# Gate and up products as three one-pass terms of split weights and input

## What is computed

```python
w = lut[idx]                                   # lut: 16 values; idx: gate, up 1376x512, down 512x1376
h = silu(x_norm @ gate.T) * (x_norm @ up.T)    # 512 positions x 1376
x = x + h @ down.T
# scan, 512 channels, 16 states, 512 steps:
state = state * exp(delta_t * A) + (delta_t * u_t) * B_t
y_t   = sum_n state[n] * C_t[n]
```

## Time and profile before

| | |
|---|---|
| median of the runs | 2582.32 us |
| the profiled execution, its own time | 2584.38 us |
| its span, first to last instruction | 2582.6 us |
| mean granted TensorE clock | 0.937 |
| busy: TensorE, VectorE, GpSimd, ScalarE | 2262.6, 1771.1, 1052.6, 920.4 us |
| window attention, about | 59 to 930 us |
| feed-forward with the scan, about | 1198 to 1865 us |

### The profile page before, as it was taken

The page is one execution under the profiler, slowest core; times in us unless marked ns, Lnnn a source line. Parts: engine busy times, 40 slices in busy tenths (PEclk is TensorE's granted clock), DMA queues, the critical chain, the costliest instruction groups (busy, mean ns, idle before and its releaser), DMA issues. The chain is left out here.

```text
span 2582.6 us, 24445 instructions
## 1 busy us (share of the span) xinstructions
PE 2262.6 (88%) x6992; PEld 1049.2 (41%) x6992; DVE 1771.1 (69%) x2979; ACT 920.4 (36%) x1759; POOL 1052.6 (41%) x789
## 2 busy tenths in 40 slices
PE   6998998999899777774798989989869999999858
PEld 3554444455455443332243434334333333434224
DVE  1887687688768877773688897987745455554454
ACT  1443323334333323331554636446203323232311
POOL 2453333355333424443598888988700000000033
PEclk9999999999999988886899999999979999999878
DMA  6000000000000022225321222221142222121021
GB/s 245 18 21 17 17 25 21 17 17 21 21 17 25 22 88 82 82 82 198 116 91 53 86 83 82 91 77 62 49 131 50 50 49 49 40 58 34 16 98 53
DMA packets 88746, 158.34 MB, mean 61 GB/s; under 512 B 14912, under 2 KB 42432, under 8 KB 86352
## 3 DMA queue, kind: packets, MB, share of 16 engines
q1 hardware_dynamic: 72256, 139.76, 17.1%
q10 hardware_dynamic: 15888, 17.43, 2.1%
q0 software_dynamic: 512, 0.13, 0.0%
HBM read 101.18 MB, written 30.80 MB: 51 GB/s over the span
## 5 line engine op out<-in xcount | busy, mean ns | idle before, releaser
L1389 PE MATMUL c_bank<-c_xn_t,c_weights 128*128 128x512 f32 (+1 forms) x704 | 326.4, 609 | 21.1 <-ACT c_h_t L1429 19.5
L706 POOL TENSOR_SCALAR a_prob<-a_prob,a_rsum 128x256 f32<-128x256 f32 x256 | 147.1, 594 | 466.8 <-DVE a_rsum L634 466.6
L1287 DVE TENSOR_TENSOR_SCAN s_state<-s_decay,s_state 128x512 f32<-128x512 f32 x256 | 305.0, 1210 | 36.1 <-ACT s_decay L1221 36.1
L1237 POOL TENSOR_TENSOR s_state<-s_b_rows,s_delta_u 128x1024 f32<-128x1024 f32 x128 | 301.2, 2363 | 11.2 <-DMA s_b_rows<-scan_bc 8.8
L1221 ACT ACTIVATE s_decay<-s_delta,s_a 128x512 f32<-128x512 f32 x256 | 173.2, 688 | 296.5 <-DVE s_state L1287 269.4
L438 PE MATMUL a_bank<-a_xn_t,a_wq 128*128 128x512 f32 x512 | 227.2, 592 | 0.0
L521 PE MATMUL a_bank<-a_wo,a_out_t 128*128 128x512 f32 x512 | 222.3, 592 | 0.0
L1910 POOL DMA_DIRECT2D d_qs<-d_neg_t x16 | 8.2, 514 | 515.3 <-DVE d_neg_t L1841 515.3
L549 ACT ACTIVATE a_prob<-a_score,a_neg_m 128x256 f32<-128x256 f32 x256 | 117.8, 476 | 278.8 <-DVE a_neg_m L629 278.6
L320 DVE TENSOR_SCALAR f_picks<-f_mask,f_lut_xor,f_lut 128x260 int32<-128x260 int32 x512 | 202.5, 468 | 9.6 <-DVE f_mask L314 1.1
L1762 ACT ACTIVATE d_prob_t<-d_score 128x512 f32<-128x512 f32 x256 | 139.0, 595 | 194.5 <-PE d_score L1645 193.2
(11 more groups left out here) (194 smaller groups left out, 3726.6 us busy)
## 6 DMA issues: line engine op xcount, KB each, us to landing
s_b_rows<-scan_bc SPq DMA_DIRECT2D x64, 512.0 KB, 3.6
f_idx<-in_idx SPq DMA_DIRECT2D x64, 130.0 KB, 2.1
ffn_weights<-f_picks SPq DMA_DIRECT2D x64, 130.0 KB, 1.8
r_factor<-in_factors SPq DMA_DIRECT2D x8, 1024.0 KB, 9.0
d_qs<-d_hi SPq DMA_DIRECT2D x128, 64.0 KB, 2.0
d_ks<-d_hi SPq DMA_DIRECT2D x128, 64.0 KB, 2.0
a_wo<-in_wo_t ACTq DMA_DIRECT2D x1, 4096.0 KB, 15.7
scan_y<-m_d_u SPq DMA_DIRECT2D x4, 1024.0 KB, 3.9
```

The lines of the kernel that those rows point to most:

```text
L1237: pool.tensor_tensor(self.state[:, s], row.broadcast_to([P, 2, T]), self.delta_u[:, h % 2], ALU.mult) \
L1287: dve.tensor_tensor_scan(self.state[:, s, e, :], self.decay[u % 2][:], self.state[:, s, e, :], 0.0, ALU.mult, ALU.add).then_inc(self.scann ...
L1389: mm = nc.tensor.matmul(banks[b][0:width[o], :], weights[:, lo:lo + width[o]], xn_t[:, k, :], start=(k == 0), stop=(k == KD - 1))
```

## The change

The lookup now stores every chunk three times: the weights, their part rounded to float32r (`f_hi`, a cast on ScalarE) and the remainder (`f_lo`, a subtraction on GpSimd). Chunks go alternately to two places; SyncE loads the indices of chunk n+1 behind the stores of chunk n-1. Gate and up indices are laid out tile by tile. In the feed-forward stage four slots hold the two parts of one gate and up tile; ScalarE issues the two loads of a tile three tiles ahead, behind silu, in every pass. Only the down weights stay in SBUF. The normalized input is split as well, a cast on ScalarE and a subtraction on VectorE per tile, and a fill is twelve one-pass products: high by high, high by low, low by high for each of four k. The next pass's normalization stands in pieces 8 and 12, among the fills, and its turning in the middle of the downs (piece 28). C of all passes is loaded and split once, into one 128-row tile.

```diff
-W_UP, W_DOWN = KD * INTER, 2 * KD * INTER
+W_DOWN = 2 * KD * INTER
...
+    STORES = 3 * 16
...
-        self.mask = sb("f_mask", [P, 4, CH], I32)
-        self.picks = sb("f_picks", [P, LUT // 2, CH], I32)
+        self.mask = sb("f_mask", [P, 3, CH], I32)
+        self.picks = sb("f_picks", [P, LUT // 2 + 1, CH], I32)
+        self.hi = sb("f_hi", [P, CH], F32R)
+        self.lo = sb("f_lo", [P, CH], F32R)
...
+    def turn(self, i, n):
+        return i * (self.PER_PASS // 2) + n // 2
+    def place(self, n):
+        return 0 if n % 2 == 0 else LUT // 2
+    def chosen(self, n):
+        return self.picks[:, self.place(n), :]
+    def scalar(self, act, i, n):
+        act.wait_ge(self.step_done, self.step_value(i, n, self.STEPS))
+        act.wait_ge(self.stored[1 - n % 2], self.turn(i, n + 1) * self.STORES + 1)
+        self.nc.scalar.copy(self.hi[:], self.chosen(n).bitcast(F32)).then_inc(self.rounded[n % 2], 1)
+    def gpsimd(self, pool, i, n):
+        pool.wait_ge(self.rounded[n % 2], self.turn(i, n) + 1)
+        self.nc.gpsimd.tensor_tensor(self.lo[:], self.chosen(n).bitcast(F32),
+                                     self.hi[:].bitcast(F32), ALU.subtract).then_inc(self.split[n % 2], 1)
...
     def sync(self, sp, i):
         def store(n):
-            sp.wait_ge(self.step_done, self.step_value(i, n, self.STEPS))
-            sp.dma_start(self.scratch["weights"][:, bass.ds(i * (self.PER_PASS * CH) + n * CH, CH)],
-                         self.picks[:, 0, :]).then_inc(self.stored, 16)
+            columns = bass.ds(i * (self.PER_PASS * CH) + n * CH, CH)
+            done = self.stored[n % 2]
+            sp.wait_ge(self.split[n % 2], self.turn(i, n) + 2)
+            sp.dma_start(self.scratch["weights"][:, columns], self.chosen(n)).then_inc(done, 16)
+            sp.dma_start(self.scratch["weights_hi"][:, columns], self.hi[:].bitcast(F32)).then_inc(done, 16)
+            sp.dma_start(self.scratch["weights_lo"][:, columns], self.lo[:].bitcast(F32)).then_inc(done, 16)
         for n in range(self.PER_PASS):
-            if n == 1:
-                sp.wait_ge(self.step_done, self.step_value(i, 0, 0))
-            elif n > 1:
-                sp.wait_ge(self.step_done, self.step_value(i, n - 2, 1))
+            if n:
+                sp.wait_ge(self.step_done, self.step_value(i, n - 1, 0))
...
+    def mask_of(self, n, bit):
+        return self.mask[:, bit, :] if bit < 3 else self.idx[:, n % 2, :]
...
             if j == 0:
-                dve.wait_ge(self.stored, (i * self.PER_PASS + n) * 16 + 1)
-            last = dve.tensor_scalar(picks[:, j, :], mask[:, 0, :], self.lut_xor[:, j:j + 1],
+                dve.wait_ge(self.stored[s], self.turn(i, n) * self.STORES + 1)
+            last = dve.tensor_scalar(picks[:, j or self.place(n), :], mask[:, 0, :], self.lut_xor[:, j:j + 1],
...
                     swap(*at, nxt[3:])
+                    lookup.scalar(act, i, g * TT)
                     take(("turn", g, 0, 0), i, prob_t[:, 0, 0, :])
                     take(("turn", g, 1, 0), i, prob_t[:, 1, 0, :])
                     take(("turn", g, 1, 1), i, prob_t[:, 1, 1, :])
@@ -591,6 +624,9 @@
                         if tt + 2 < TT:
                             for prev in range(2):
                                 take(("turn", g, tt + 2, prev), i, prob_t[:, tt % 2, prev, :])
+                        if tt % 2 == 0:
+                            lookup.scalar(act, i, g * TT + 1 + tt // 2)
+                    lookup.scalar(act, i, g * TT + 3)
...
+                    for n in range(TT):
+                        lookup.gpsimd(pool, i, g * TT + n)
...
+        for row in range(0, P, DS):
+            sp.dma_start(self.c_raw[row:row + DS, :], self.scratch["bc"][row // DS % B, DS:2 * DS, :]) \
+                .then_inc(self.c_in, 16)
...
+        n = c // 32 * DS + c % 16
+        self.nc.tensor.matmul(self.c_bank[c % 2][:], self.c_pick[:, n:n + 1].broadcast_to([P, P]),
+                              self.c_parts[:], start=True, stop=True).then_inc(self.c_spread, 1)
...
+    SLOTS = 4
+    w_parts = sb("c_w_parts", [P, SLOTS, 2, 2 * KD * P], F32R)
+    w_down = sb("c_w_down", [P, OT, D], F32)
...
-    xn_t = sb("c_xn_t", [P, KD, T], F32)
+    xn_parts = sb("c_xn_parts", [P, 2, KD, T], F32R)
...
+    PARTS = len(SPLIT)
+    XN_AT = FILLS + 2 * PARTS
+    PIECES = FILLS + TT * PARTS + 1
+    USES = OT + TT // 2 + KD // 2
+    STATS_AT, NORM_AT = 8, 12
...
+    def load_weights(eng, i, o):
+        n = i * OT + o
+        s, columns = n % SLOTS, slice(o * 2 * KD * P, o * 2 * KD * P + 2 * KD * width[o])
+        for part, name in enumerate(("weights_hi", "weights_lo")):
+            eng.dma_start(w_parts[:, s, part, 0:2 * KD * width[o]].bitcast(F32), scratch[name][:, columns]) \
+                .then_inc(w_in[s], 16)
...
-                for k in range(KD):
-                    lo = b * W_UP + k * INTER + o * P
-                    mm = nc.tensor.matmul(banks[b][0:width[o], :], weights[:, lo:lo + width[o]], xn_t[:, k, :],
-                                          start=(k == 0), stop=(k == KD - 1))
+                terms = [(k, w, x_) for k in range(KD) for w, x_ in ((0, 0), (0, 1), (1, 0))]
+                for k, w, x_ in terms:
+                    at = (b * KD + k) * width[o]
+                    mm = nc.tensor.matmul(banks[b][0:width[o], :], w_parts[:, n % SLOTS, w, at:at + width[o]],
+                                          xn_parts[:, x_, k, :],
+                                          start=((k, w, x_) == terms[0]), stop=((k, w, x_) == terms[-1]))
...
+                    elif j == XN_AT:
+                        if i + 1 < B:
+                            features(i + 1)
+                    else:
+                        down(i, *down_piece(j))
...
+            def load_ahead(n):
+                if n < B * OT:
+                    if n >= SLOTS:
+                        i, o = divmod(n - SLOTS, OT)
+                        act.wait_ge(full[1], fill_turn(i, o) + 1)
+                    load_weights(act, *divmod(n, OT))
+            for n in range(1, SLOTS):
+                load_ahead(n)
...
+                        if i * OT + j // 2 >= 1:
+                            load_ahead(i * OT + j // 2 + SLOTS - 1)
+                    if j == XN_AT and i + 1 < B:
...
+            def features(i):
+                for k in range(KD):
+                    dve.wait_ge(xn_rounded, i * KD + k + 1)
+                    nc.vector.tensor_tensor(xn_parts[:, 1, k, :], banks[k % 2][:], xn_parts[:, 0, k, :].bitcast(F32),
+                                            ALU.subtract).then_inc(free[k % 2], 1)
```

More of the change, by code:

```diff
@@ L262, in __init__ @@
         self.step_done = core.sem("f_step")
-        self.stored = core.sem("f_stored")
+        self.rounded = core.sems("f_rounded", 2)
+        self.split = core.sems("f_split", 2)
+        self.stored = core.sems("f_stored", 2)
     def load_table(self, sp):
@@ L291, in sync_end @@
     def sync_end(self, sp):
-        sp.wait_ge(self.stored, 16 * CHUNKS + 1)
+        for done in self.stored:
+            sp.wait_ge(done, self.STORES * (CHUNKS // 2) + 1)
     def vector_setup(self, dve):
-        start_at_one(dve, self.step_done, self.stored)
+        start_at_one(dve, self.step_done, *self.stored, *self.split)
         dve.wait_ge(self.lut_in, 16)
@@ L313, in pick @@
         for bit in range(1, 4):
-            last = dve.tensor_scalar(mask[:, bit, :], self.idx[:, s, :], 1 << bit, None, ALU.bitwise_and)
+            last = dve.tensor_scalar(self.mask_of(n, bit), self.idx[:, s, :], 1 << bit, None, ALU.bitwise_and)
         last.then_inc(self.step_done, 1)
@@ L329, in choose @@
             for j in range(0, LUT // 2, 2 * half):
-                last = self.nc.vector.copy_predicated(self.picks[:, j, :], self.mask[:, level + 1, :],
+                last = self.nc.vector.copy_predicated(self.picks[:, j or self.place(n), :], self.mask_of(n, level + 1),
                                                       self.picks[:, j + half, :])
@@ L1124, in load_half @@
         sp.dma_start(self.delta_u[:, s], self.scratch["delta_u"][i, :, own, :]).then_inc(self.delta_u_in[s], 16)
-        if h % 2 == 0:
-            if i:
-                sp.wait_ge(self.c_split, i)
-            for part in range(2):
-                sp.dma_start(self.c_raw[part * DS:(part + 1) * DS, :], self.scratch["bc"][i, DS:2 * DS, :]) \
-                    .then_inc(self.c_in, 16)
     def load_rows(self, sp, r):
@@ L1202, in scalar_setup @@
         act.wait_ge(self.pick_in, 16)
-        self.nc.scalar.copy(self.c_pick[:], self.pick_raw[:, 0:DS]).then_inc(self.picked, 1)
-        self.round_c(act, 0)
+        self.nc.scalar.copy(self.c_pick[:], self.pick_raw[:, 0:B * DS]).then_inc(self.picked, 1)
+        act.wait_ge(self.c_in, P // DS * 16)
+        self.nc.scalar.copy(self.c_hi[:], self.c_raw[:]).then_inc(self.c_rounded, 1)
         act.wait_ge(self.a_step, 2)
-    def round_c(self, act, i):
```

(33 more changed lines are left out.)

81 lines of the change are left out of this document (32 added, 49 removed).

## The result

| | |
|---|---|
| median of the runs after | 2609.72 us, four runs (2608.64 to 2611.96) |
| before, beside them | 2582.06 us (2578.64 to 2584.28) |
| ratio | 1.0109, 95% interval 1.0092 to 1.0127 |
| span of the profiled execution | 2606.9 us (before 2582.6) |
| mean granted TensorE clock | 0.927 (before 0.937) |

The changed kernel is slower by some 27 us. Two large amounts of opposite sign make that up. I read them from the first instruction of each stage: the context stage begins at 1028.0 in place of 930.6 us, so window attention takes **97.4 us more**. From the first statistics of the feed-forward stage to the first of the stage behind it are 615.3 us in place of 684.1, so that stage takes **68.8 us less**. The remaining stages together take 4.3 us less. Nothing was done to find out why.

A forecast was written before the change was run, and what follows sets the result against it. TensorE was taken as the bound, alternating with ScalarE in attention and matched by an equal scalar chain in feed-forward fills. 58 + 8 + 28 - 8 - 24 - 19 = +43 gave 2625 us for the median, range 2570 to 2670.

The forecast's parts named there:

- The new wait of ScalarE: Attention: ScalarE's cast of chunk 1 waits for VectorE and delays TensorE; +58 us in twelve groups, +8 in three normalizing ones.
- Clock: Attention: twelve new TensorE stalls are each followed by a lower granted clock, 2.3 us lost each, +28 us.
- The rest of the lookup: Attention: GpSimd's 64 subtractions and 128 more stores hide behind other work, costing nothing.
- One-pass fills: Feed-forward gate and up: TensorE saves 0.64 us per fill, but the scalar chain stays; -8 us, last pass only.
- one chain: Feed-forward fills: ScalarE's exp, table loads and silu, then the scans, hold a pair with two chunks at 8.1 us.
- Downs: Feed-forward downs of three passes: normalization leaves, 11 us less each, transposes cost 3 more; -24 us.
- start: Feed-forward start: fewer loads on ScalarE's queue ahead of the first decay, first fill some 4 us later; -19 us.
- C spread: Feed-forward: 128 rows in place of 32 stream the same 512 columns, one split replaces four; costed at nothing.
- A: Rival, attention: cast, subtraction, stores and index load close too late, so VectorE waits as well; 2670 us, chance 0.14.
- B: Rival, feed-forward fills: TensorE is the bound, so its saving is paid in full; 2562 us, faster, chance 0.09.
- C: Rival, attention: ScalarE's holds do not reach TensorE, only 64 casts cost time; 2556 us, faster, chance 0.08.
- D: Rival, fills: a one-pass product costs 0.43 us, weight loads not hidden; 2625 + 100 us, chance 0.05.

The follow-up runs named there:

- experiments 1 and 3: experiment 1, and as third the kernel before with ScalarE only waiting for chunks 1 and 2, no cast, subtraction or store added: 2664.36 us, ratio 1.0309.
- experiment 1: The changed kernel with the casts of chunks 1 to 3 of each group moved behind the group's last copy on ScalarE: 2535.89 us, ratio 0.9829.

## Why the prediction came out as it did

2625 us was forecast and 2609.7 measured: slower, as forecast, and inside the range. 43 us more was forecast, 27.7 measured. By its steps:

- **The new wait of ScalarE** (58 + 8). Right in place and kind, as experiments 1 and 3 show. TensorE's idle time grew by 68.2 us, against 66. The parts are less good than the sum. The hold, its cast included, was taken as 7.7 and 5.6 us by turns, and is about 7.6 in every plain group (645.74 to 653.32 in the one shown), of which TensorE feels 5.6 to 5.8; so the plain groups cost 68.5 us in place of 58. The three others cost 28.7, less the 19.6 of late adds: 9, against 8. Against that stand 11.8 us less of waits for GpSimd's probabilities, which the prediction did not have. So the close sum is in part luck.
- **Clock** (+28). 27.9 us more of busy TensorE for the same work. The mechanism is in the rows behind the hold; the size per hold was 2.7 us in the one shown, against 2.3, and there were fifteen holds and not twelve, while stalls of before went. That the total agrees is luck too. Idle time and clock together, 68.2 + 27.9 = 96.1, are the 96 us by which the window of the stage grew.
- **The rest of the lookup** (nothing). Wrong: the step said that 64 subtractions hide because GpSimd is busy for only 341 of 871 us. They hide on GpSimd; on VectorE they cost 20 us in experiment 1. How much of it the changed kernel feels beside its holds was not separated.
- **One-pass fills** (0 for three passes, -8 for the last). The last came out at -10.7. The two in the middle were forecast at 97 and took 90; pass 0's, forecast near 100, took 94. This is the term that was mis-sized, by 12.9 us in the two middle passes alone: it carried the normalization over from the downs at 7.4 us, its length beside a busy GpSimd, and it took 1.9. The other part are the DMA issues, 0.3 us in each of nine pairs, 2.7 us a pass, that cost nothing. 97 - 5.5 - 2.7 = 88.8, against 90.0; 88 - 2.7 = 85.3, against 85.8.
- **Why the fills do not go lower.** The prediction named one chain. Its length was right and its rank was not: the chain without its table loads frees 4 us by the medians, TensorE with a third of its products and a lower clock 10, and both 20; in the last pass GpSimd holds then.
- **Downs** (-24) came out at -26, **start** (-19) at +6.4 - 25.7 = -19.3. That last agreement is in part luck: the first fill waited 6.4 us longer and not 4, and the fills of pass 0 gained 6.4 us with those of the other passes, which the prediction had at nothing. The **C spread** came out at nothing: a product of 128 rows has a median of 499 ns, one of 32 rows had 492.
- **Rivals.** A's closing chain did not appear: none of VectorE's 64 first mask instructions (L343) is found waiting for its indices. B did not come to pass, since TensorE is idle for 11 of 90 us. C is refuted by the 100 us in which TensorE waits for ScalarE. D is refuted by 2.96 us for twelve products.

In all, 66 + 28 + 0 - 8 - 24 - 19 = 43 was forecast; 97.4 - 68.8 - 4.3 = 24.3 was found. Attention was 3 us over its terms, the feed-forward stage 18 us under, 12.9 of it in the two middle phases of fills.

## What to carry to other kernels

Before an instruction is put into an engine's list, look up what stands behind it there and who waits for that; fifteen waits of 7 to 11 us between two copies (and as many shorter ones behind them) cost 86 us here, and with the casts behind the last copy the attention lost 21 us in place of 97. Two chains that are equally long in the trace say nothing of what either would give: shorten each alone, then both, and look whether TensorE's clock fell with its work. A duration on VectorE is worth no more than the GpSimd rows beside it, so a step that is moved is costed by what runs in its new place.

## What was not expected of the hardware

- One normalizing VectorE instruction of 128x512 took 0.54 us with GpSimd idle. In the downs of before, where operations of 2.4 us ran on GpSimd, nine of twelve took 1.97 to 2.56 us.
- TensorE with a third of its products in the fills was granted a clock of 0.66 in place of 1.00, and its product of 512 columns that spreads C had a median of 793 in place of 500 ns.
- GpSimd was busy for 391 of 891 us in the attention of experiment 1, and still 64 subtractions there of 0.80 us, in place of 0.25, took 0.31 us each from VectorE.
- ScalarE's queue issued two DMAs while the activation before them and even a table load ran, ahead of the silu that stands before them in the list: 0.78 us of issuing for nothing. A table load was followed by its activation after 0.01 us here too (1527.57 + 1.28, then 1528.86); the Trainium skill's drain of about 1380 ns (ScalarE: Activation LUTs, What ACT_TABLE_LOAD costs) did not show in it.
- The two switches of activation table per pair, 2.56 us of 8.1, are worth 3.7 us over the whole kernel by the medians, and 6.2 us of the feed-forward stage, when everything else stays.
